# A cross-attention and soft-MoE kernel: the context turned on VectorE in 32x32 blocks instead of on TensorE

## The chip, the cores and the metric

One core of a Trainium2 chip runs the whole kernel in one launch. The metric is device time in microseconds (us): the median of three executions. TensorE (PE) multiplies and transposes into PSUM, VectorE (DVE) and ScalarE (ACT) work on PSUM and SBUF, GpSimd (POOL) on SBUF only, and SyncE (SP) issues transfers. All of them run in their own order and meet at semaphores.

## The reference, cut to what matters

```python
# x: (8, 56, 128), ctx_1024: (8, 1500, 128); 16 heads of 64
def _L0_xattn_ref(x, context, Wq, Wk, Wv, Wo):
    q = (x @ Wq).reshape(B, N, HEADS, DIM_HEAD)
    k = (context @ Wk).reshape(B, M, HEADS, DIM_HEAD)
    v = (context @ Wv).reshape(B, M, HEADS, DIM_HEAD)
    attn = jax.nn.softmax(jnp.einsum('bihd,bjhd->bhij', q, k) * SCALE, axis=-1)
    out = jnp.einsum('bhij,bjhd->bihd', attn, v).reshape(B, N, INNER)
    return out @ Wo
...
x = x + _L0_xattn_ref(_layernorm(x), ctx_1024, ...)   # attention over 1500 keys
x = x + _L0_ffn_ref(_layernorm(x), ...)               # soft mixture of 64 experts, 32 slots each
```

## The kernel before, in words

Keys are never projected: the weights of the query and key side are folded into one matrix per head, so that the scores of a batch are (folded queries) x (context turned). For a batch the 16 heads x 56 tokens are 896 rows, seven tiles of 128. The main loop runs over eight batches `b` and seven steps `t` of one tile each; `g = 7 b + t`. All float32 products are made of a high and a low part in the faster fp32r type: high x high, high x low, low x high. So the context is needed in four forms:

- `ctx_th`, `ctx_tl` (128 features x 1500 keys, high and low), for the scores, with keys along the free dimension;
- `ctx_nh`, `ctx_nl` (125 partitions x 12 chunks x 128 features), for the product of probabilities and context.

Both come from `ctx_raw`, which holds one batch in its natural layout: partition p has the 12 keys 12p to 12p + 11, 6144 bytes in one run (`ctx_v`). TensorE turns it in `turn_ctx`, three times four chunks, into a bank of `misc`; ScalarE copies the high part out (`hi_ctx`, L973), VectorE subtracts for the low part (`lo_ctx`, L1207), and the next four chunks wait for that (`ctxT_lo`). For batch `b + 1` this happens in steps 1, 2, 3 of batch `b`. GpSimd makes the natural parts in `split_ctx` (L408 and L412), one instruction each.

A step goes like this. TensorE makes the scores of tile g (L605 to L607), which must wait for the exponential of tile g - 1 since there is one scores buffer; turns two thirds of the probabilities of tile g - 1 (L617); does some chunks of the product with the context (`context_product`, L637 to L639, as `share` deals them out: groups of tiles (0,1), (2,3,4), (5,6)); turns the last third; and does the extras of `end_step`. VectorE takes row maxima (L1221, L1224), subtracts for the low part of the turned probabilities (`lo_probs`, L1231), inverts row sums (`invert`, L1240) and normalises a finished group (`normalise`, L1256). ScalarE copies high parts (`hi_probs`, L988), and takes the exponential (L995).

The one accumulator bank `acc` serves all groups, so a new group waits for `normalise` of the last (`oT_dve`). `normalise` needs the reciprocal row sums as a row on every partition, `rbc`. They take a path over DRAM, on SP's queue: `spread_rden` waits for `invert`, writes `rden_row` (L356), waits for it to land, waits for the normalisation before, and reads it back broadcast to 128 partitions (L359). VectorE normalises group 0 of batch b in step 6, group 1 in step 1 of batch b + 1, group 2 in step 3, each ahead of the row maxima of that step. SP runs in this order, with the load of the natural context between two spreadings:

```python
for b in range(B):
    if b > 0:
        spread_rden(NG * b, (b + 1) % 2, 2)
    spread_rden(NG * b + 1, b % 2, 0)
    if b + 2 < B:
        load_ctx(b + 2)
    spread_rden(NG * b + 2, b % 2, 1)
```

`load_ctx(b)` waits until `ctx_raw` is free, that is until TensorE has turned batch b - 1 and GpSimd has split it (`ctx_nat >= b`). The feed-forward part of the pairs of batches that are finished runs in between (`ffn_step`, `mid_step`, `dispatch_*`, `combine_*`), and its rest, with the experts, after the last batch.

## Time and profile before

| | |
|---|---|
| median of three executions | 452.91 us (450.67 to 454.25) |
| the profiled execution | 450.83 us, span 448.8 us |
| TensorE, VectorE, ScalarE, GpSimd busy | 96%, 76%, 55%, 31% of the span |
| granted TensorE clock | full, 1.0 in every slice |
| DMA | 19.05 MB, 42 GB/s over the span |

The span is the time from the first to the last instruction that the profiler recorded, and the execution is 2.0 us longer. Busy shares are of the whole span; the eight batches take the time from about 22 to 391 us, and the rest belongs to the start and to the experts. A row of the timeline has a start, a duration, the engine, the line, the operation, and in brackets how long the engine had been idle before it and what ended that.

### The profile page before, as it was taken

What the parts mean: (1) busy time and instruction counts of PE and PEld (TensorE: products, weight loads), DVE (VectorE), ACT (ScalarE), POOL (GpSimd) and SP (SyncE); (2) the same over time, 40 slices, a digit from 0 to 9 for tenths busy, and PEclk for the clock granted to TensorE, in tenths of its full rate; (3) what the DMA queues carried; (4) which work ended last, traced back from release to release, by engine and by line L of the source; (5) the groups of instructions that cost most, each with busy time, mean ns of one, the idle gap of its engine ahead of it and who ended that gap; (6) DMA issues with size and microseconds to landing.
All of it is one profiled execution on the core that took longest, in us unless ns stands there. A gap on an engine that the chain in (4) does not pass through costs nothing.

```text
span 448.8 us, 7525 instructions
## 1 busy us (share of the span) xinstructions
PE 429.8 (96%) x3038; PEld 392.6 (87%) x3038; DVE 339.1 (76%) x620; ACT 247.1 (55%) x422; POOL 137.5 (31%) x75
## 2 busy tenths in 40 slices
PE   1899999999999999999999999999999999899997
PEld 1788899999999999889999998989999888898986
DVE  2367776887587768757898778988997999668871
ACT  1375556665665356554665566646755654633641
POOL 1408100503050005030624043264440343446740
PEclk9999999999999999999999999999999999999999
DMA  7162110111001001110020011000100000576000
GB/s 224 52 143 34 65 25 12 13 68 19 13 13 70 19 12 14 68 19 13 9 73 19 12 13 69 19 1 15 14 18 2 12 13 23 90 193 183 1 3 20
DMA packets 15110, 19.05 MB, mean 42 GB/s; under 512 B 3954, under 2 KB 10882, under 8 KB 15076
## 3 DMA queue, kind: packets, MB, share of 16 engines
q1 hardware_dynamic: 13604, 16.48, 14.8%
q10 hardware_dynamic: 1472, 2.10, 1.6%
q8 instruction: 24, 0.39, 0.4%
q14 instruction: 10, 0.08, 0.1%
HBM read 18.32 MB, written 0.26 MB: 41 GB/s over the span
## 4 chain that ended last, share of the span: by engine, by line
PE 77%; DVE 10%; ACT 5%; DMA 3%; issue 2%; POOL 2%; POOLq 1%; SPq 0%
PE turned L617 15%; PE scores L605 8%; PE acc L639 8%; PE acc L637 8%; PE acc L638 8%; PE scores L607 8%; PE scores L606 8%; PE misc L654 3%; PE misc L549 3%; DMA ctx_raw<-in_ctx_dram 3%; DVE small L1221 2%; PE misc L679 2%; DVE pT_l L1231 2%; PE misc L543 2%; ACT prob L995 2%
## 5 line engine op out<-in xcount | busy, mean ns | idle before, releaser
L988 ACT CAST pT_h<-turned 125x512 fp32r<-125x512 f32 x168 | 94.9, 589 | 122.4 <-PE turned L617 121.7
L1231 DVE TENSOR_TENSOR pT_l<-turned,pT_h 125x512 fp32r<-125x512 f32 x168 | 112.2, 686 | 59.5 <-ACT pT_h L988 58.8
L1221 DVE TENSOR_REDUCE small<-scores 128x1 f32<-128x500 f32 x168 | 109.2, 674 | 10.2 <-PE scores L607 10.1
L617 PE MATMUL turned<-ident,prob 128*125 128x128 f32 x672 | 94.7, 276 | 2.8 <-DVE pT_l L1231 2.6
L617 PEld LDWEIGHTS turned<-ident,prob 128*125 128x125 f32 x672 | 87.5, 187 | 10.5 <-DVE pT_l L1231 4.3
L637 PE MATMUL acc<-pT_h,ctx_nh 125*128 125x256 f32 (+1 forms) x288 | 94.6, 329 | 0.0
L995 ACT ACTIVATE prob<-scores,small 128x1500 f32<-128x1500 f32 x56 | 84.9, 1516 | 14.5 <-DVE small L1224 14.5
L639 PE MATMUL acc<-pT_h,ctx_nl 125*128 125x256 f32 (+1 forms) x288 | 86.5, 300 | 0.0
L638 PE MATMUL acc<-pT_l,ctx_nh 125*128 125x256 f32 (+1 forms) x288 | 86.3, 300 | 0.0
L605 PE MATMUL scores<-ctx_th,qk_h 128*128 128x500 f32 x168 | 68.2, 406 | 0.7 <-DVE qk_l L1214 0.3
L607 PE MATMUL scores<-ctx_th,qk_l 128*128 128x500 f32 x168 | 65.3, 389 | 0.0
L606 PE MATMUL scores<-ctx_tl,qk_h 128*128 128x500 f32 x168 | 65.0, 387 | 0.0
L408 POOL TENSOR_TENSOR ctx_nh<-ctx_raw,zero 125x1536 fp32r<-125x1536 f32 x8 | 22.0, 2746 | 113.6 <-PE acc L639 98.9
L638 PEld LDWEIGHTS acc<-pT_l,ctx_nh 125*128 125x128 f32 x288 | 54.6, 190 | 0.0
L637 PEld LDWEIGHTS acc<-pT_h,ctx_nh 125*128 125x128 f32 x288 | 54.6, 189 | 0.0
L639 PEld LDWEIGHTS acc<-pT_h,ctx_nl 125*128 125x128 f32 x288 | 54.4, 189 | 0.0
L607 PEld LDWEIGHTS scores<-ctx_th,qk_l 128*128 128x128 f32 x168 | 31.5, 188 | 6.5
L605 PEld LDWEIGHTS scores<-ctx_th,qk_h 128*128 128x128 f32 x168 | 31.6, 188 | 6.3 <-issue 1.7
L606 PEld LDWEIGHTS scores<-ctx_tl,qk_h 128*128 128x128 f32 x168 | 31.7, 189 | 4.4
L458 POOL TENSOR_TENSOR logit<-logit,cmax 112x2048 f32<-112x2048 f32 (+1 forms) x5 | 18.5, 3704 | 34.1 <-DVE cmax L1287 32.5
L412 POOL TENSOR_TENSOR ctx_nl<-ctx_raw,ctx_nh 125x1536 fp32r<-125x1536 f32 x8 | 27.8, 3479 | 0.6
L419 POOL TENSOR_TENSOR qk_h<-qk_raw,zero 128x896 fp32r<-128x896 f32 x4 | 6.7, 1679 | 56.3 <-DVE qk_l L1214 56.3
(166 smaller groups left out, 537.3 us busy)
## 6 DMA issues: line engine op xcount, KB each, us to landing
ctx_raw<-in_ctx_dram SPq DMA_DIRECT2D x7, 750.0 KB
rbc<-rden_row SPq DMA_DIRECT2D x15, 128.0 KB, 3.4
rbc<-rden_row SPq DMA_DIRECT2D x8, 192.0 KB, 3.0
eb<-in_L_ffn_expert_b_dram SPq DMA_DIRECT2D x4, 256.0 KB, 6.1
ctx_raw<-in_ctx_dram SPq DMA_DIRECT2D x3, 250.0 KB
wq_sb<-in_L_xattn_Wq_dram ACTq DMA_DIRECT2D x1, 512.0 KB, 4.9
wk_sb<-in_L_xattn_Wk_dram ACTq DMA_DIRECT2D x1, 512.0 KB, 8.1
wv_sb<-in_L_xattn_Wv_dram ACTq DMA_DIRECT2D x1, 512.0 KB, 9.0
```

Of the source, the lines that this page charges most:

```text
L412: gp.tensor_tensor(ctx_nl[a][:, :, :], ctx_raw[:, :, :], ctx_nh[a][:, :, :].bitcast(F32), ALU.subtract).then_inc(ctx_nat, 1)
L605: mm(o, hi, ctx_th[a][:, keys], start=True, stop=False)
L606: mm(o, hi, ctx_tl[a][:, keys], start=False, stop=False)
L607: mm(o, lo, ctx_th[a][:, keys], start=False, stop=True).then_inc(scores_pe, 1)
L617: last = tr(turned[0:CK, m, 128 * c:128 * c + 128], prob[u][:, CK * j:CK * j + CK], ident[:, :])
L637: mm(o, ctx_nh[a][:, j, :], hi, start=(j == 0), stop=False)
L638: mm(o, ctx_nh[a][:, j, :], lo, start=False, stop=False)
L639: last = mm(o, ctx_nl[a][:, j, :], hi, start=False, stop=(j == NC - 1))
L988: nc.scalar.copy(pT_h[0:CK, PLACES[g // NT % 2][t], CPB * k:CPB * k + CPB, :], turned[0:CK, (KB * u + k) % 2, :].rearrange("p (c r) -> p c ...
L995: nc.scalar.activation(prob[u][:, :].rearrange("p (k w) -> p k w", k=KB), scores[:, :, 0:KW], ACT.Exp, bias=negmax[:, u:u + 1], accum_out= ...
L1221: m = v.tensor_reduce(bankmax[:, u, k:k + 1], scores[:, k, 0:KW], AX.X, ALU.max)
L1231: v.tensor_tensor(pT_l[0:CK, place, dst, :], turned[0:CK, (KB * u + k) % 2, :].rearrange("p (c r) -> p c r", c=CPB), pT_h[0:CK, place, dst ...
```

## The change

For batches 1 to 7 the context is turned in another way. A second load (`load_blocks`) brings the same batch once more from DRAM, laid out by blocks: partition 32e + k holds, for each block n of 32 keys, the 32 features 32e to 32e + 31 of key 32n + k. That is a run of 128 bytes for each partition and block. Eight DMAs do it: for each e one of 46 blocks (1472 runs) and one of the last block (32 runs), which overlaps the block before by four keys. VectorE's transpose of 32x32 blocks then gives the turned context, `ctx_tf`, in SBUF: four instructions for a batch, in steps 1, 2 and 3 of the batch before. ScalarE casts all 1500 columns to `ctx_th` in one instruction after step 4 (`hi_ctx`), and GpSimd subtracts for `ctx_tl` in one (`lo_ctx`), which lies ahead of `split_ctx` of the same batch in its order. The block loads of batches 2 to 7 are issued by ScalarE (`next_blocks`), behind that cast (batch 7's at the end of step 6 of batch 5); batch 1's by SP at the start.

Keys are now numbered straight, so the natural load of batches 1 to 7 takes another layout: partition p holds the keys 125j + p, 12 runs of 512 bytes (`ctx_c`). Batch 0 is as before. `ctx_tf` uses the memory of `ctx_tl`, and the block buffers lie in buffers of the feed-forward part, which adds two waits (`dispatch_shift(1)` for the last transposes, `logits(2, 0)` for the copies of the logits before).

```diff
+        ctx_tf = [at("ctx_tf0", [D, M], F32, tl0_at), at("ctx_tf1", [D, M], F32, tl1_at)]
+        BLK = 32
+        NB = -(-M // BLK)
+        blocks_at = [None] + [disp0_at + 1024] * 4 + [logit1_at] * 2 + [wqk_at]
...
+        ctx_c = ctx_1024.rearrange("b (j p) d -> b p j d", j=NC)
+
+        def load_blocks(eng, b):
+
+            for e in range(D // BLK):
+                cols = slice(BLK * e, BLK * e + BLK)
+                whole = ctx_1024[b, 0:BLK * (NB - 1), cols].rearrange("(n k) d -> k n d", k=BLK)
+                eng.dma_start(ctx_blk[b][cols, 0:NB - 1, :], whole).then_inc(blk_in, 16)
+                eng.dma_start(ctx_blk[b][cols, NB - 1, :], ctx_1024[b, M - BLK:M, cols]).then_inc(blk_in, 16)
...
             def load_ctx(b):
-                sp.wait_ge(ctxT_pe, KB * b)
+                sp.wait_ge(ctxT_pe, KB)
                 sp.wait_ge(ctx_nat, b)
-                sp.dma_start(ctx_raw[:, :, :], ctx_v[b]).then_inc(ctx_in, 16)
+                sp.dma_start(ctx_raw[:, :, :], ctx_c[b]).then_inc(ctx_in, 16)
...
+            load_blocks(sp, 1)
             load_ctx(1)
...
+            def lo_ctx(b):
+
+                pool.wait_ge(ctxT_hi, KB + b)
+                a = b % 2
+                gp.tensor_tensor(ctx_tl[a][:, :], ctx_tf[a][:, :], ctx_th[a][:, :].bitcast(F32),
+                                 ALU.subtract).then_inc(ctxT_lo, 1)
...
             def dispatch_shift(q):
                 pool.wait_ge(dmax_dve, 2 * (q + 1))
+                if q == 1:
+                    pool.wait_ge(ctxT_dve, B - 1)
...
-            split_ctx(1, 1)
...
+            lo_ctx(1)
+            split_ctx(1, 1)
+            lo_ctx(2)
             split_ctx(2, 0)
             split_qk(1)
+            lo_ctx(3)
             split_ctx(3, 1)
             root(1, 0, 1)
+            lo_ctx(4)
             split_ctx(4, 0)
...
             def end_step(b, t):
 
                 i, a, q = b // 2, b % 2, (b - 4) // 2
-                if 1 <= t <= 3 and b < B - 1:
-                    if t > 1:
-                        pe.wait_ge(ctxT_lo, KB * (b + 1) + t - 1)
-                    elif b == 2:
-                        pe.wait_ge(phi_cp, 1)
-                    elif b in (4, 6):
-                        pe.wait_ge(logit_act, LC * (q + 1))
-                    turn_ctx(b + 1, t - 1, 0)
...
                     if t == 0:
-                        pe.wait_ge(ctxT_lo, KB * (b + 1))
+                        pe.wait_ge(ctxT_lo, KB + b)
...
+            def hi_ctx(b):
+
+                act.wait_ge(ctxT_dve, b)
+                nc.scalar.copy(ctx_th[b % 2][:, :], ctx_tf[b % 2][:, :]).then_inc(ctxT_hi, 1)
+
+            def next_blocks(b):
+
+                if b == B - 1:
+                    act.wait_ge(qk_pe, 4 * PAIRS)
+                else:
+                    act.wait_ge(ctxT_dve, b - 1)
+                load_blocks(act, b)
...
-                if 1 <= t <= 3 and b < B - 1:
-                    hi_ctx(b + 1, 1 - a, t - 1, 0)
+                if t == 4 and b < B - 1:
+                    hi_ctx(b + 1)
+                if t == 4 and b < B - 3:
+                    next_blocks(b + 2)
+                if (b, t) == (B - 3, 6):
+                    next_blocks(B - 1)
...
+            def turn_blocks(b, part):
+
+                dst = ctx_tf[b % 2]
+                if part == 0:
+                    dve.wait_ge(blk_in, blocks_loaded(b))
+                    v.transpose(dst[:, M - BLK:M], ctx_blk[b][:, NB - 1, :]).then_inc(last_blk, 1)
+                n0, n1 = 16 * part, min(16 * part + 16, NB - 1)
+                if part == 2:
+                    dve.wait_ge(last_blk, b)
+                m = v.transpose(dst[:, BLK * n0:BLK * n1], ctx_blk[b][:, n0:n1, :].rearrange("p n d -> p (n d)"))
+                if part == 2:
+                    m.then_inc(ctxT_dve, 1)
...
-                    if 2 <= t <= 4 and b < B - 1 and not first:
-                        lo_ctx(b + 1, 1 - a, t - 2, 0)
+                    if 1 <= t <= 3 and b < B - 1:
+                        turn_blocks(b + 1, t - 1)
```

## Rows read from the trace of the kernel before

**Rows 1.** The page's chain of work that ended last, by engine.
```profile
PE 77%; DVE 10%; ACT 5%; DMA 3%; issue 2%; POOL 2%; POOLq 1%; SPq 0%
```

**Rows 2.** Timeline of TensorE's weight loads, end of step 1 of batch 2.
```profile
121.18 0.46 PEld L543 LDWEIGHTS misc<-ident,ctx_raw 125*128 125x128 f32 x4
...
121.61 0.47 PEld L662 LDWEIGHTS misc<-ident,phi_sb 128*128 128x128 f32 x4
```

**Rows 3.** Timeline of VectorE and ScalarE, step 1 of batch 3.
```profile
161.32 0.65 DVE L1256 TENSOR_TENSOR oT<-acc,rbc 128x384 f32<-128x384 f32 x1
...
163.95 1.51 ACT L995 ACTIVATE prob<-scores,small 128x1500 f32<-128x1500 f32 x1 [0.27 <-DVE small L1224]
```

**Rows 4.** TensorE's timeline: starts of step 4 and next step 2, batches 0, 2, 5.
```profile
45.35 0.46 PE L605 MATMUL scores<-ctx_th,qk_h 128*128 128x500 f32 x1
...
77.05 0.47 PE L605 MATMUL scores<-ctx_th,qk_h 128*128 128x500 f32 x1
...
133.80 0.47 PE L605 MATMUL scores<-ctx_th,qk_h 128*128 128x500 f32 x1
...
166.38 0.47 PE L605 MATMUL scores<-ctx_th,qk_h 128*128 128x500 f32 x1
...
271.75 0.48 PE L605 MATMUL scores<-ctx_th,qk_h 128*128 128x500 f32 x1
...
306.77 0.47 PE L605 MATMUL scores<-ctx_th,qk_h 128*128 128x500 f32 x1
```

**Rows 5.** Groups of instructions: busy us, mean ns of one, idle before, releaser.
```profile
L408 POOL TENSOR_TENSOR ctx_nh<-ctx_raw,zero 125x1536 fp32r<-125x1536 f32 x8 | 22.0, 2746 | 113.6 <-PE acc L639 98.9 <-DMA ctx_raw<-in_ctx_dram 14.8
L412 POOL TENSOR_TENSOR ctx_nl<-ctx_raw,ctx_nh 125x1536 fp32r<-125x1536 f32 x8 | 27.8, 3479 | 0.6
...
L1207 DVE TENSOR_TENSOR ctx_tl<-misc,ctx_th 128x500 fp32r<-128x500 f32 x24 | 16.0, 668 | 6.1 <-ACT ctx_th L973 6.1
```

**Rows 6.** Timeline of two DMA issues: start, time that the queue is held.
```profile
2.17 0.76 ACTq L958 DMA_DIRECT2D wo_sb<-in_L_xattn_Wo_dram  x1
...
24.49 0.82 SPq L365 DMA_DIRECT2D phi_sb<-in_L_ffn_phi_w_dram  x1
```

**Rows 7.** ScalarE's timeline, steps 4 and 5 of batches 2 and 4.
```profile
138.57 1.06 ACT L988 CAST pT_h<-turned 125x512 fp32r<-125x512 f32 x2
143.27 0.58 ACT L988 CAST pT_h<-turned 125x512 fp32r<-125x512 f32 x1 [3.64 <-PE turned L617]
...
231.45 1.93 ACT L1034 ACTIVATE disp<-disp 112x2048 f32<-112x2048 f32 x1
235.21 0.58 ACT L988 CAST pT_h<-turned 125x512 fp32r<-125x512 f32 x1 [1.83 <-PE turned L617]
```

**Rows 8.** SP's timeline in batch 2: the context load, then group 1's sums.
```profile
134.36 0.28 SPq L348 DMA_DIRECT2D ctx_raw<-in_ctx_dram  x1
144.69 0.32 SPq L356 DMA_DIRECT2D rden_row<-small  x1
```

**Rows 9.** Windows: length, engines' busy time, clock, DMA share of 16 engines, GB/s.
```profile
28.00:30.00 2.00, 2.00 (x12) 1.70 (x11) 1.61 (x4) 0.36 (x2) 0.00 (x0) 1.00 1.06 207
...
34.00:36.00 2.00, 2.00 (x15) 1.77 (x14) 2.00 (x5) 0.58 (x1) 0.86 (x1) 1.00 0.33 97
...
140.00:142.00 2.00, 2.00 (x14) 1.77 (x14) 0.98 (x2) 0.00 (x0) 0.00 (x0) 1.00 0.29 120
...
397.00:402.00 5.00, 5.00 (x49) 5.00 (x49) 3.22 (x6) 1.05 (x3) 1.32 (x2) 1.00 1.05 304
```

**Rows 10.** DMA issues of the page: count, KB each, median us to landing.
```profile
rbc<-rden_row SPq DMA_DIRECT2D x15, 128.0 KB, 3.4
...
rden_row<-small SPq DMA_DIRECT2D x15, 1.0 KB, 3.0
...
phi_sb<-in_L_ffn_phi_w_dram SPq DMA_DIRECT2D x1, 0.5 KB, 12.5
```

**Rows 11.** ScalarE's timeline, step 5 of batch 0: first work after step 4's copies.
```profile
52.86 0.60 ACT L973 CAST ctx_th<-misc 128x500 fp32r<-128x500 f32 x1
```

More of the change, by code:

```diff
@@ L133, in xattn_softmoe_kernel @@
         ctx_th1, t1_at = take("ctx_th1", [D, M], F32R)
-        ctx_tl1, _ = take("ctx_tl1", [D, M], F32R)
+        ctx_tl1, tl1_at = take("ctx_tl1", [D, M], F32R)
         qk_h1, _ = take("qk_h1", [D, HEADS, T], F32R)
@@ L137, in xattn_softmoe_kernel @@
         ctx_th0, t0_at = take("ctx_th0", [D, M], F32R)
-        ctx_tl0, _ = take("ctx_tl0", [D, M], F32R)
+        ctx_tl0, tl0_at = take("ctx_tl0", [D, M], F32R)
         qk_h0, _ = take("qk_h0", [D, HEADS, T], F32R)
@@ L156, in xattn_softmoe_kernel @@
         disp0, disp0_at = take("disp0", [PT, SLOTS])
-        logit1, _ = take("logit1", [PT, SLOTS])
+        logit1, logit1_at = take("logit1", [PT, SLOTS])
         _, stat0_at = take("stat0", [PT, 96])
@@ L181, in xattn_softmoe_kernel @@
         comb = logit
+        ctx_tf = [at("ctx_tf0", [D, M], F32, tl0_at), at("ctx_tf1", [D, M], F32, tl1_at)]
+        BLK = 32
+        NB = -(-M // BLK)
+        blocks_at = [None] + [disp0_at + 1024] * 4 + [logit1_at] * 2 + [wqk_at]
+        ctx_blk = [blocks_at[b] and at(f"ctx_blk{b}", [D, NB, BLK], F32, blocks_at[b]) for b in range(B)]
         stats_at = [stat0_at, stat1_at, t0_at + 2 * KB8, t0_at + 2 * KB8 + 384]
@@ L222, in xattn_softmoe_kernel @@
         ctxT_pe = sem("ctxT_pe")
+        blk_in = sem("blk_in")
+        ctxT_dve = sem("ctxT_dve")
+        last_blk = sem("last_blk")
         ctxT_hi = sem("ctxT_hi")
@@ L498, in _ @@
             dispatch_shift(0)
+            lo_ctx(5)
             split_ctx(5, 1)
@@ L501, in _ @@
             root(2, 1, 2)
+            lo_ctx(6)
             split_ctx(6, 0)
@@ L506, in _ @@
             dispatch_shift(1)
+            lo_ctx(7)
             split_ctx(7, 1)
@@ L534, in _, with turn_ctx @@
             tr = nc.tensor.transpose
-            def turn_ctx(b, k, m, first=False):
-                if first:
-                    pe.wait_ge(ctx0_in[k], 16)
-                else:
-                    pe.wait_ge(ctx_in, 16 * b)
+            def turn_ctx(k, m):
+                pe.wait_ge(ctx0_in[k], 16)
                 for c in range(CPB):
@@ L572, in _ @@
             turn_weight(wq_sb, 1, S1)
-            turn_ctx(0, 0, 1, first=True)
+            turn_ctx(0, 1)
             pe.wait_ge(xn_ready, 1)
@@ L577, in _ @@
             last.then_inc(setup_pe, 1)
-            turn_ctx(0, 1, 0, first=True)
+            turn_ctx(1, 0)
             pe.wait_ge(wk_in, 16)
@@ L582, in _ @@
             pe.wait_ge(ctxT_lo, 1)
-            turn_ctx(0, 2, 1, first=True)
+            turn_ctx(2, 1)
             pe.wait_ge(setup_dve, 3)
@@ L700, in mid_step @@
                     pe.wait_ge(x2nT_act, 3)
+                    pe.wait_ge(logit_act, 2 * LC)
                     logits(2, 0)
@@ L729, in end_step @@
                 if b in (3, 5) and t == 4:
-                    pe.wait_ge(ctxT_lo, KB * (b + 2))
+                    wait(pe, logit_act, LC * (i - 1))
                     pe.wait_ge(x2nT_act, i)
@@ L812, in half @@
                             head_products(wvT, wo_sb, 1, ACC)
[L813 to L815 removed]
+                            pe.wait_ge(qk_lo, 4)
                             head_products(wvT, wo_sb, 3, M1)
@@ L967, in copy_out, with hi_ctx0 @@
                 return nc.scalar.copy(dst, blocks4(bank(k))).then_inc(setup_act, 1)
-            def hi_ctx(b, a, k, m):
-                act.wait_ge(ctxT_pe, KB * b + (k + 1))
-                nc.scalar.copy(ctx_th[a][:, KW * k:KW * k + KW], misc[:, m, 0:KW]).then_inc(ctxT_hi, 1)
+            def hi_ctx0(k, m):
+                act.wait_ge(ctxT_pe, k + 1)
+                nc.scalar.copy(ctx_th[0][:, KW * k:KW * k + KW], misc[:, m, 0:KW]).then_inc(ctxT_hi, 1)
+            def hi_ctx(b):
[7 more added lines that the diff above has]
+                load_blocks(act, b)
             def hi_qk(i, r, m):
@@ L1113, in _ @@
             copy_out(2, wqT[:, 4:8, :], S1)
-            hi_ctx(0, 0, 0, 1)
-            hi_ctx(0, 0, 1, 0)
+            hi_ctx0(0, 1)
+            hi_ctx0(1, 0)
             copy_out(5, wkT[:, 4:8, :], T0)
-            hi_ctx(0, 0, 2, 1)
+            hi_ctx0(2, 1)
             copy_out(6, wqk[:, 0:8:2, :], T1, SCALE)
```

29 lines of the change are left out of this document (10 added, 19 removed).

## The prediction, made before the changed kernel had run

> **What bounds the kernel now.** I read the page's chain of work first: 77% of the chain that ended last is on TensorE [rows 1], and the page has it busy almost throughout. Work taken off TensorE is therefore worth its own time, as long as the other engines keep up. Next the timeline of one step (a "step" is one of the seven 128-row tiles of a batch, counted 0 to 6, batches 0 to 7). A group of four context transposes starts at 121.18 us and the next group of weight loads at 121.61: 0.43 us of TensorE's time, with no gap around it [rows 2]. Then the waits near the batch boundary, since that is where the change moves things: in step 1 of batch 3 VectorE normalises group 1 of batch 2 at 161.32, then takes the row maxima, and ScalarE's exponential starts 2.63 us after it, at 163.95 [rows 3]. The scores of step 2 overwrite the scores the exponential reads, and start at 166.38 [rows 4]. So that tile has about 0.9 us of slack (163.95 + 1.51 = 165.46). Last the DMA queues, because two new loads and one changed load use them.
>
> **What is saved.** In batches 1 to 6, steps 1 to 3 each lose four transposes: 18 x 0.43 = 7.7 us. In batch 0 the chain runs through VectorE and ScalarE; its copies of the low part (0.67 us each [rows 5], in steps 2, 3, 4) move to the middle of the step, where VectorE waits for the exponential. I count 0.6 us each, of which two lie ahead of the point I measure from below: 1.2 us.
>
> **VectorE.** 21 subtractions of 0.668 us go, 21 block transposes of 448 or 512 columns and 7 of 32 come. No row shows a VectorE transpose. The nearest is the subtraction that goes, 0.668 us for 500 columns [rows 5]; I bound it by half of that and by double. I take the same rate, 0.65 us, and 0.15 for the short one, so VectorE's work stays within 0.1 us a batch, and it stands where VectorE waits for the exponential anyway. At double it would cost perhaps 0.3 us in the fullest steps, some 2 us in all; at half it gives nothing, as VectorE is not the bound there. The Trainium skill (Vector Engine (DVE) Microarchitecture Reference, section 3.8) says that the transpose sustains one element per cycle per lane; by that the 512 columns would be an estimated 0.53 us plus overhead. No run here shows it yet.
>
> **ScalarE.** 21 copies out of PSUM become 7 casts of 1500 columns from SBUF, about 1.5 us each (2048 columns took 1.93 us [rows 7]), at the end of step 4. Behind each stand eight DMA issues on ScalarE's queue. Nearest rows: 0.76 and 0.82 us for loads of several runs per partition [rows 6], 0.28 and 0.32 us for plain ones [rows 8]. I take 4 x (0.75 + 0.32) = 4.3 us; bounds 2.3 and 6.6. Queued behind them are the next high-part copy (143.27 in batch 2, after 3.64 us without work) and, in batch 4, a 1.93 us exponential that starts at 231.45 while the next copy starts at 235.21 [rows 7]. With issues and cast overlapping, the copy is late by roughly 0.4 us in batch 2, 2.1 in batch 4, 1.2 to 1.5 in batches 0, 1, 3, and nothing in batch 5, where the next step has room. Alone that would be 6.7 us, since these steps have four chunks of product, which just cover the copy.
>
> **GpSimd and the SP queue; here the change hurts.** The low part of batch b+1 goes onto GpSimd *ahead* of the split of batch b+1. In batch 2:
> - Step 4 starts at 133.80 [rows 4]; ScalarE's last copy of it ends at 138.57 + 1.06 = 139.63 [rows 7], 5.8 us into the step. The cast ends at 7.3.
> - The low part on GpSimd: 3.48 us for 1536 columns [rows 5], 3.4 for 1500: 10.7. Then the split, 2.75 + 3.48 [rows 5]: 17.1.
> - SP's next load of the natural context waits for that split. In the old kernel it was issued at 134.36 [rows 8], 0.6 into step 4; now at 17.1.
> - Directly behind it on SP stands the spreading of the reciprocal sums of group 1, which was issued at 144.69, ten us *after* the load. Now it is issued just after it.
> - The load keeps five engines of sixteen busy: the DMA share is 0.29 while it runs, with 120 GB/s, until about 142 [rows 9]. A transfer queued behind such a load waits for those five: the phi load, 1 MB issued at 24.49 directly behind batch 1's context load, took 12.5 us to land [rows 6, 10]; the share fell from 1.06 to 0.33, five engines, for its last part [rows 9].
> - The new load has 1500 runs of 512 bytes, 300 for each of five engines. The expert load's runs are 512 bytes: 304 GB/s on sixteen engines [rows 9] is 27 ns a run and engine. 300 x 27 = 8.1 us, and 0.9 us before the first byte: it ends at 26.1 after step 4's start. Bounds: 21 ns (120 GB/s on five engines) and 40 ns (207 GB/s, the phi load), so 6.4 to 12 us.
> - The 1 KB of reciprocals lands in 3.0 us from its issue, the broadcast back in 3.4 [rows 10]. The first is already issued, so +2.1, then +3.4: 31.6.
> - VectorE wants it at 161.32, which is 27.5 after step 4's start. It waits 4.1 us, in order, ahead of the row maxima. The exponential ends 2.6 + 1.5 later, and the scores of step 2 start 0.2 after: 35.9.
>
> Before, those scores started 166.38 - 133.80 = 32.6 after step 4's start: +3.3. The same two rows of each batch (the first, third and last of six are in [rows 4]) give spans of 31.7, 32.0, 32.6, 35.0, 32.9 and 35.0 us for batches 0 to 5. In batch 0 ScalarE is free only 7.5 into the step [rows 11], so 37.6 stands against 31.7. The shifts: +5.9, +3.9, +3.3, +0.9, +3.0, +0.9 = +17.9 us. They contain the late copies of ScalarE (the late broadcast outlasts them, except for 0.3 in batch 3) and the lost transposes of step 1. Batches 6 and 7 have no such load.
>
> The engine count is where the Trainium skill bears on this (DMA: Bandwidth & Descriptors, "Why a DMA increments its semaphore by 16 and not by 1"): a transfer takes the largest number of engines up to 16 that divides the slowest dimension of both sides. For 125 partitions that is 5, also in the new layout; the share of 0.29 to 0.33 [rows 9] agrees for the old one (five sixteenths are 0.31). With sixteen engines the forecast would be the first rival below.
>
> **The block loads.** A batch is 6016 runs of 128 bytes, 376 an engine. The rows of 512-byte runs, 27 and 40 ns [rows 9], bound it above, and a quarter of 27 for a quarter of the bytes bounds it below: 3 to 15 us. Batches 2 to 6 have over 20 us. Batch 7's is issued at about 292 and wanted at about 305, batch 1's waits behind batch 0's load until about 17 and is wanted at 31: up to 25 or 30 ns nothing, at 40 about 3 us each. I take none.
>
> **Sum.** +17.9 - 1.2 - 12 x 0.43 (steps 2 and 3) = +11.5; with 0.3 of ScalarE and a few tenths where VectorE becomes the tighter engine, +12. The profiled execution took 450.83 us (span 448.8), 2.1 under the median of 452.91. 450.8 + 12 = 463 for such an execution, 465 as a median.
>
> **Rivals.**
> 1. *The broadcast comes in time*: the new load spreads over sixteen engines, or the small transfers don't queue behind it. Then it is ready 5.6 us earlier, at 26, and only batch 0 is short by 1 us. For it: the new source pattern has never run. Against: the share rows and the phi load. With cheap issues on ScalarE (2.6 us, as the 0.32 us rows, late copies of about 1 us in all): 450.8 - 9.5 + 2 = 443, median 445. This is the case on the other side; it decides from a broadcast ready before 27.5.
> 2. *The same, with ScalarE's issues at 0.75 us for the wide ones*: -9.5 + 6.7 + 1 = -2, median 451.
> 3. *Dearer runs*: 40 ns for 512 bytes adds 3.9 us to each of six batches: +23, and some 3 us of late blocks: 488 to 491. The row for it is the phi load, which however ran beside another load.
> 4. *Eight DMAs in a row are more than the queue takes*, and ScalarE is held while blocks move. The loads of the start and of phi never stand more than four in a row on a queue. Four wide transfers of 2.5 us would hold it 10 us a batch: about 495.
>
> **Chances.** Forecast 0.62 (456 to 476), rival 1 0.15, rival 2 0.10, rival 3 0.09, rival 4 0.04. The measurement can tell about 1%, 4.5 us. Rival 1 is faster by over 1%, rival 2 within it, the rest slower; with a little of the forecast's lower tail within: 0.16, 0.12, 0.72. The range from 447 to 487 leaves out most of rival 1 and the upper cases, about 2 in 10.
>
> **What would show it.** In the changed kernel's waits: VectorE's normalisation waiting for the broadcast in step 1 of batches 1 to 6, some 4 us, less in batches 4 and 6; SP's context load issued 17 us into step 4's span; DMA share about 0.31 for some 8 us with the reciprocals landing only after it, 10 us or more instead of 3. ScalarE's eight issues summing to about 4.3 us; transposes near 0.65 us; TensorE busy about 11 us less (84 transposes) in a longer span. The prediction is wrong if normalisation does not wait: then either the engine count or the queue order was misread. It is too low if VectorE waits for blocks.

## The result, and the profile after

The changed kernel takes 479.76 us (median of four executions, 478.53 to 481.13) against 453.52 us before in the same comparison: the ratio is 1.059, with a 95% interval of 1.0535 to 1.065. The profiled executions stand at 481.13 us (span 479.3) and 450.83 us (span 448.8), so this pair differs by 30.5 us of span; the pair is accounted for below. The forecast had +12. (Single executions of the kernel before differ by up to 4 us, and the profiled one is among its fastest; by the medians the change costs 26.2 us.)

The chain of work that ended last, by engine; against [rows 1] TensorE has gone from 77% to 34%, and waiting for issues, transfers and other engines has come in:

```profile
PE 34%; issue 18%; DVE 16%; DMA 9%; ACT 9%; POOL 8%; ACTq 4%; POOLq 1%; SPq 0%
```

To see where, I took from TensorE's timeline the first scores row of each step in both kernels (L605 before, L640 after, as in [rows 4]) and subtracted the lengths of the steps. The first scores of all start at 26.16 us instead of 22.43 (+3.7). Then, after minus before, in us:

| batch | step 0 | 1 | 2 | 3 | 4 | 5 | 6 | sum |
|---|---|---|---|---|---|---|---|---|
| 0 | +0.3 | 0.0 | 0.0 | -0.6 | -0.8 | +0.8 | 0.0 | -0.3 |
| 1 | 0.0 | **+6.7** | 0.0 | -0.4 | -0.1 | **+1.7** | 0.0 | +7.9 |
| 2 | 0.0 | **+5.8** | -0.3 | -0.4 | +0.1 | +1.1 | 0.0 | +6.3 |
| 3 | 0.0 | +1.8 | -0.4 | -0.4 | -0.1 | +1.3 | 0.0 | +2.1 |
| 4 | 0.0 | -0.4 | -0.4 | +0.3 | +0.1 | **+3.7** | 0.0 | +3.4 |
| 5 | 0.0 | -0.2 | -0.4 | -0.4 | -0.1 | 0.0 | 0.0 | -1.1 |
| 6 | **+7.2** | +1.4 | -0.4 | +0.1 | +0.1 | 0.0 | 0.0 | +8.4 |

Batch 7 and everything behind it are unchanged. The steps that shrink by 0.4 are those that lost a group of transposes [rows 2]. The rest are four places, and each has its rows.

**Step 1: the broadcast is late.** GpSimd's timeline at the end of batch 0 (low part, then the two halves of the split), SP's, and VectorE's and TensorE's in step 1 of batch 1, then of batch 2:

```profile
57.12 3.41 POOL L441 TENSOR_TENSOR ctx_tl<-ctx_tf,ctx_th 128x1500 fp32r<-128x1500 f32 x1 [12.69 <-ACT ctx_th L1000]
60.48 2.75 POOL L430 TENSOR_TENSOR ctx_nh<-ctx_raw,zero 125x1536 fp32r<-125x1536 f32 x1
63.31 3.49 POOL L434 TENSOR_TENSOR ctx_nl<-ctx_raw,ctx_nh 125x1536 fp32r<-125x1536 f32 x1
...
66.87 0.30 SPq L369 DMA_DIRECT2D ctx_raw<-in_ctx_dram  x1
67.21 5.99 SPq L377 DMA_DIRECT2D rden_row<-small  x1
76.87 0.32 SPq L380 DMA_DIRECT2D rbc<-rden_row  x1
...
81.57 0.66 DVE L1307 TENSOR_TENSOR oT<-acc,rbc 128x384 f32<-128x384 f32 x1 [5.98 <-DMA rbc<-rden_row]
82.38 0.55 PE L672 MATMUL acc<-pT_h,ctx_nh 125*128 125x256 f32 x1 [4.68 <-DVE oT L1307]
87.21 0.62 PE L640 MATMUL scores<-ctx_th,qk_h 128*128 128x500 f32 x1
...
132.84 0.66 DVE L1307 TENSOR_TENSOR oT<-acc,rbc 128x384 f32<-128x384 f32 x1 [5.16 <-DMA rbc<-rden_row]
133.65 0.55 PE L672 MATMUL acc<-pT_h,ctx_nh 125*128 125x256 f32 x1 [3.45 <-DVE oT L1307]
139.19 0.61 PE L640 MATMUL scores<-ctx_th,qk_h 128*128 128x500 f32 x1
```

The context load is issued the moment the split ends, 66.87, and the reciprocals directly behind it. The 5.99 on that row is not the transfer: it is how long the *issue* holds SP's queue, where the same instruction took 0.32 in [rows 8]. The load's own runs of 512 bytes are on the engines from 0.94 to 9.23 us after its issue. The broadcast is there at 81.57, 14.7 us after the load was issued, and VectorE and then TensorE stand idle for it. VectorE waits so in three batches only: 5.98 us in step 1 of batch 1, 5.16 in batch 2, 2.44 in batch 3. In batches 4, 5 and 6 its wait there is 0.08, 0 and 0.

**What the stall does to TensorE's clock.** Windows over step 1 of batch 2 (columns: length; busy time of PE, PEld, DVE, ACT, POOL; granted clock; DMA share; GB/s):

```profile
128.00:130.00 2.00, 2.00 (x14) 1.77 (x13) 0.00 (x0) 0.20 (x1) 0.00 (x0) 1.00 0.11 43
130.00:132.00 2.00, 0.20 (x2) 0.01 (x1) 0.00 (x0) 0.39 (x1) 0.00 (x0) 1.00 0.18 56
132.00:134.00 2.00, 0.35 (x1) 0.38 (x2) 1.16 (x2) 0.00 (x0) 0.00 (x0) 0.66 0.00 0
134.00:136.00 2.00, 2.00 (x11) 2.00 (x11) 1.97 (x6) 0.51 (x1) 0.00 (x0) 0.50 0.08 28
136.00:138.00 2.00, 2.00 (x11) 2.00 (x11) 1.16 (x4) 1.57 (x3) 0.00 (x0) 0.50 0.11 38
138.00:140.00 2.00, 2.00 (x11) 1.92 (x10) 0.99 (x2) 1.01 (x2) 0.00 (x0) 0.63 0.03 8
```

In and after 3.45 us of idleness the engine is granted 0.50, the lower of its two levels (1.2 of 2.4 GHz), and works at it for about 6 us. From the normalisation to the next scores it takes 139.19 - 132.84 = 6.35 us here and 5.64 in batch 1. In batch 3, where VectorE waits only 2.4 us and the column stays at 1.00, it is 4.3.

**Step 5: ScalarE's issues.** ScalarE's timeline in batch 4, the last of eight issues and the exponential behind them, which stood at 231.45 before, directly behind its predecessor [rows 7]:

```profile
250.11 0.32 ACTq L324 DMA_DIRECT2D ctx_blk<-in_ctx_dram  x1
...
254.12 0.82 ACTq L325 DMA_DIRECT2D ctx_blk<-in_ctx_dram  x1
254.99 1.91 ACT L1069 ACTIVATE disp<-disp 112x2048 f32<-112x2048 f32 x1 [2.33 <-issue]
...
314.34 1.52 ACTq L325 DMA_DIRECT2D ctx_blk<-in_ctx_dram  x1
...
316.36 5.78 ACTq L325 DMA_DIRECT2D ctx_blk<-in_ctx_dram  x1
...
323.87 2.51 ACTq L325 DMA_DIRECT2D ctx_blk<-in_ctx_dram  x1
326.41 0.59 ACT L1058 COPY logit<-misc 112x512 f32<-112x512 f32 x1 [11.85 <-issue]
```

The eight take 4.83 us (250.11 to 254.94). L324 is the wide issue, 1472 runs, and L325 the one of 32 runs behind it; even unhindered the small one takes longer (0.71 to 0.91 us, the wide one 0.32 to 0.45).

In batch 4 TensorE has 1.98 us without work behind this, and the clock falls there too, which is part of the +3.7:

```profile
258.00:260.00 2.00, 1.84 (x12) 1.84 (x13) 2.00 (x3) 1.84 (x4) 1.92 (x2) 0.73 0.00 0
260.00:262.00 2.00, 2.00 (x11) 2.00 (x11) 1.97 (x2) 0.00 (x0) 2.00 (x1) 0.50 0.03 8
```

**Step 0 of batch 6: ScalarE held.** The second part of the fence with ScalarE's issues is batch 7's blocks, issued by ScalarE at 314 while SP's context load (issued at 310.93) is in flight. Two of the small issues, each behind a wide one, are held 5.78 and 2.51 us, and ScalarE does nothing for 11.85 us. VectorE, which needs its copies, waits 9.02, and TensorE 6.07 and runs at 0.50 afterwards.

**The start.** SP's timeline (batch 1's blocks right behind batch 0's context) and TensorE's; two rows of before follow for comparison:

```profile
3.10 10.01 SPq L325 DMA_DIRECT2D ctx_blk<-in_ctx_dram  x1
...
17.69 1.07 PE L578 MATMUL misc<-ident,ctx_raw 125*128 125x125 f32 x4 [0.53 <-DMA ctx_raw<-in_ctx_dram]
...
19.92 0.42 PE L600 MATMUL turned<-wkT,wqT 64*128 64x128 f32 x1
```

```profile
16.80 0.84 PE L543 MATMUL misc<-ident,ctx_raw 125*128 125x125 f32 x4
...
18.79 0.27 PE L565 MATMUL acc<-wkT,wqT 64*128 64x128 f32 x1
```

The third part of batch 0's context comes 0.9 us later. The rest of the +3.7 is TensorE's clock: from the first of the L600 rows to the first scores it takes 7.5 us, where it took 4.9 before, and the same product has rows of 0.42 us against 0.27. The clock column prints 1.00 for both, but it has nothing to go by there. The trace's first entry on the clock, a rise to 1.00, is at 26.83 us in the changed kernel and at 17.27 in the kernel before. That the rows ahead of it are at the lower level shows by their length. Sixteen matmuls of one shape, first in the changed kernel's start and in the start of the kernel before, then in the changed kernel at a granted 0.50 (15 records) and at 1.00:

```profile
22.73 3.75 PE L584 MATMUL misc<-xnT,wqk 128*128 128x112 f32 x16
```

```profile
20.11 2.01 PE L549 MATMUL misc<-xnT,wqk 128*128 128x112 f32 x16 [0.28 <-issue]
```

```profile
259.13 3.36 PE L689 MATMUL misc<-oT,wvo 128*128 128x112 f32 x15
...
353.57 1.94 PE L689 MATMUL misc<-oT,wvo 128*128 128x112 f32 x16
```

Why the clock rises 9.6 us later in one kernel than in the other stays open: none of the runs below settles it.

### The profile page after: what moved, and what is told of

Read it like the earlier page. It is cut to its first block, busy times and chain, and to the rows that moved or that the text cites. A ratio compares the mean times of both kernels' runs of the same rounds, so it can differ in the third digit from the quotient of the medians.

```text
span 479.3 us, 7399 instructions
## 1 busy us (share of the span) xinstructions
PE 436.6 (91%) x2954; PEld 396.6 (83%) x2954; DVE 339.0 (71%) x627; ACT 245.8 (51%) x408; POOL 161.0 (34%) x82
## 4 chain that ended last, share of the span: by engine, by line
PE 34%; issue 18%; DVE 16%; DMA 9%; ACT 9%; POOL 8%; ACTq 4%; POOLq 1%; SPq 0%
PE turned L652 6%; DVE small L1272 5%; DVE pT_l L1282 5%; DMA rden_row<-small 4%; ACT prob L1030 4%; PE scores L640 3%; ACTq L325 3%; DMA ctx_raw<-in_ctx_dram 3%; PE scores L642 3%; PE scores L641 3%; PE acc L672 3%; PE acc L674 3%; PE acc L673 3%; ACT pT_h L1023 3%; PE misc L689 3%
## 5 line engine op out<-in xcount | busy, mean ns | idle before, releaser
L652 PE MATMUL turned<-ident,prob 128*125 128x128 f32 x672 | 96.5, 280 | 16.6 <-DVE pT_l L1282 16.2
L652 PEld LDWEIGHTS turned<-ident,prob 128*125 128x125 f32 x672 | 88.8, 190 | 26.0 <-DVE pT_l L1282 20.6
L672 PE MATMUL acc<-pT_h,ctx_nh 125*128 125x256 f32 (+1 forms) x288 | 96.7, 336 | 9.2 <-DVE oT L1307 9.2
L674 PE MATMUL acc<-pT_h,ctx_nl 125*128 125x256 f32 (+1 forms) x288 | 88.3, 307 | 0.0
L673 PE MATMUL acc<-pT_l,ctx_nh 125*128 125x256 f32 (+1 forms) x288 | 88.1, 306 | 0.0
L441 POOL TENSOR_TENSOR ctx_tl<-ctx_tf,ctx_th 128x1500 fp32r<-128x1500 f32 x7 | 23.9, 3413 | 176.1 <-ACT ctx_th L1000 176.1
L640 PE MATMUL scores<-ctx_th,qk_h 128*128 128x500 f32 x168 | 69.2, 412 | 1.0 <-ACT prob L1030 0.7
L672 PEld LDWEIGHTS acc<-pT_h,ctx_nh 125*128 125x128 f32 x288 | 56.3, 196 | 9.7 <-issue 9.7
L673 PEld LDWEIGHTS acc<-pT_l,ctx_nh 125*128 125x128 f32 x288 | 56.4, 196 | 0.0
L674 PEld LDWEIGHTS acc<-pT_h,ctx_nl 125*128 125x128 f32 x288 | 56.2, 195 | 0.0
L640 PEld LDWEIGHTS scores<-ctx_th,qk_h 128*128 128x128 f32 x168 | 32.6, 194 | 7.2 <-issue 2.0
L468 POOL TENSOR_TENSOR disp<-logit,dmax 112x2048 f32<-112x2048 f32 x3 | 11.0, 3650 | 40.3 <-DVE ctx_tf L1257 25.1
```

Source lines behind the costliest of these rows:

```text
L640: mm(o, hi, ctx_th[a][:, keys], start=True, stop=False)
L652: last = tr(turned[0:CK, m, 128 * c:128 * c + 128], prob[u][:, CK * j:CK * j + CK], ident[:, :])
L672: mm(o, ctx_nh[a][:, j, :], hi, start=(j == 0), stop=False)
L673: mm(o, ctx_nh[a][:, j, :], lo, start=False, stop=False)
L674: last = mm(o, ctx_nl[a][:, j, :], hi, start=False, stop=(j == NC - 1))
```

## The experiments

All are edits of the changed kernel unless said otherwise. "Excess" is the length of a step over before, as in the table above. Each time stands beside runs of the kernel before (medians 453.5 to 454.0).

### e1_spread_first: SP's two orders exchanged

```diff
                 spread_rden(NG * b + 1, b % 2, 0)
+                spread_rden(NG * b + 2, b % 2, 1)
                 if b + 2 < B:
                     load_ctx(b + 2)
-                spread_rden(NG * b + 2, b % 2, 1)
```

> The changed kernel with one change of order on SP: the spreading of group 1's reciprocals goes ahead of the load of the natural context. Theory A (the broadcast of group 1 is late because it queues behind the context load): step 1 of batches 1 to 3 and 6 loses its excess over the old kernel (6.7, 5.8, 1.8 and 1.4 us in the trace of the changed kernel) and the steps 1 of all six batches show the 0.4 us of the transposes saved; no normalisation waits for the broadcast for more than 1 us. That is 17 to 18 us: 462 us from 479.8. The 7.2 us in step 0 of batch 6 stay, since batch 7's blocks still collide with a context load. Theory B (the DMA issues on ScalarE are the main cost, and the wait for the broadcast is only where it shows): the lost time moves to the next wait, and the time stays above 474.

459.72 us, ratio 1.016 [1.0105, 1.021]. Step 1 of batches 1 to 3 went from +6.7, +5.8, +1.8 to -0.35, -0.43, -0.35: the whole stall there, and the clock's fall with it, were the order on this queue. Steps 5 kept +0.8, +1.6, +1.2, +1.2, +3.9, step 0 of batch 6 kept +5.2 and its step 1 +0.6, where the saving was expected too. Two lines are worth 20 us.

### e2_split_first: GpSimd's split ahead of its low part

```diff
-            lo_ctx(2)
             split_ctx(2, 0)
+            lo_ctx(2)
```

(for each batch, with the other extras in place)

> The changed kernel with GpSimd's order turned round: the split of a batch goes ahead of its low part, so that SP's context load is issued again in step 4 or before. Theory A: the broadcast is in time in all batches, worth 17 to 18 us, and batch 7's blocks no longer meet a context load, worth 7 more: 455. Theory B (a queue that issues is held while a context load fills the rings): now every block load of batches 2 to 6 is issued some 5 us behind a context load instead of 5 us ahead of one, so ScalarE is held about 5 us in step 4 of each batch and the gain is eaten: 475 to 485.

488.59 us, ratio 1.079 [1.073, 1.086]: worse, as the second theory had it, and by more than its 475 to 485. The steps 1 and step 0 of batch 6 are repaired, but the context load now goes out just ahead of ScalarE's block loads, and steps 5 have +7.3, +7.9, +7.9, +7.3, +9.1. Each of the five has a gap of 5.6 to 7.4 us in TensorE's work and 6.8 us at a granted 0.50. SP's and ScalarE's timeline in batch 4:

```profile
253.99 0.28 SPq L369 DMA_DIRECT2D ctx_raw<-in_ctx_dram  x1
...
258.17 1.38 ACTq L325 DMA_DIRECT2D ctx_blk<-in_ctx_dram  x1
...
260.06 5.60 ACTq L325 DMA_DIRECT2D ctx_blk<-in_ctx_dram  x1
...
268.14 1.91 ACT L1069 ACTIVATE disp<-disp 112x2048 f32<-112x2048 f32 x1 [7.78 <-issue]
```

The load is on SP's queue and the held issue on ScalarE's. What they share, as far as the trace shows it, are the engines that move the data. It is not that only one queue can issue at a time: in the changed kernel SP's issue is held from 311.65 to 318.51, and ScalarE gets three issues through meanwhile. The start is that of the changed kernel, yet here the clock is up at 18.68 and the first scores are 1.1 us late, not 3.7.

### e3_load_16_engines: the context load cut into 112 + 13 partitions

```diff
-                sp.dma_start(ctx_raw[:, :, :], ctx_c[b]).then_inc(ctx_in, 16)
+                sp.dma_start(ctx_raw[0:112, :, :], ctx_c[b][0:112]).then_inc(ctx_in, 16)
+                sp.dma_start(ctx_raw[112:CK, :, :], ctx_c[b][112:CK]).then_inc(ctx_in, 16)
```

> The changed kernel with the natural context load in two parts, 112 and 13 partitions, in place of one of 125; the order of everything stays. Theory A (the load keeps five engines busy for 8.3 us, since it has 125 partitions): 112 partitions are spread over sixteen engines, the load takes about 3 us, the DMA share is near 1 while it runs, the broadcast comes 5 us earlier, and the waits for it fall from 6.0 to about 1 us: some 13 us, and several us less of the hold in step 0 of batch 6: 460 to 465. Theory B (the broadcast is late because of the 1500 short runs as such, on whatever engines): no more than 3 us are gained.

461.84 us, ratio 1.021 [1.015, 1.026]. Step 1 has +3.1 in batch 1, its saving in batches 2 to 5, and +0.4 in batch 6; step 0 of batch 6 falls from +7.2 to +2.3. A window of the load shows what the cut does, 0.36 and 107 GB/s in the changed kernel (first), 0.86 and 182 here:

```profile
70.00:72.00 2.00, 2.00 (x16) 1.96 (x15) 1.78 (x4) 1.20 (x2) 0.00 (x0) 1.00 0.36 107
```

```profile
70.00:72.00 2.00, 2.00 (x16) 1.96 (x15) 1.78 (x4) 1.14 (x2) 0.00 (x0) 1.00 0.86 182
```

So the number of engines set the length of the load, as the prediction read it. What is left in batch 1 is plain queueing without a held issue: the reciprocals are issued at 68.07 in 0.37 us and the broadcast can only follow at 73.87.

### e4_start_later: batch 1's blocks after batch 0's context

```diff
+            for k in range(KB):
+                sp.wait_ge(ctx0_in[k], 16)
             load_blocks(sp, 1)
```

> The changed kernel with batch 1's block load issued by SP only when the three parts of batch 0's context have landed (about 17 us). Theory A (the 3.7 us by which the first scores start later, 26.2 against 22.4, come from the block load that shares the engines with the first context parts and the weights, after which TensorE's matmuls run longer for some microseconds): the first scores start near 22.5 us again and the whole kernel gains 3 to 4 us, 476. Theory B (the start is slower for another reason, or VectorE then waits for batch 1's blocks in step 1 of batch 0 for as long): no change, 479 to 481.

476.67 us, ratio 1.053 [1.047, 1.058]; the first scores come 0.25 us later than before's instead of 3.7. The transfers account for about 1 us of that (the third part is turned at 16.97 instead of 17.69); the rest is TensorE's clock, which is up at 17.62 here, so that the L600 rows are at 0.27 us. In this profile step 5 of batch 4 has +2.1 in place of +3.7: TensorE's gap is the same 2.0 us there, but the clock stays at 1.00 behind it.

### e11_change_again: the changed kernel once more

No edit.

> The changed kernel once more, unaltered, for the start: its profile showed TensorE's rows between 18 and 26 us of the span 1.57 times as long as before's (0.42 against 0.27 us), the kernel with the later start showed them at 0.27. Theory A (the longer rows belong to this kernel): first scores again 3.7 us late, 478.5 to 481. Theory B (they belong to single executions): first scores 1.1 us late in this profile, and a time of 477.

479.52 us, first scores again 3.8 us late, rows again at 0.42, the clock's rise at 26.57. So the late rise is no accident of one execution. It is not fixed by what the kernel does at the start either. The profile of e2 has the changed kernel's start and its rise at 18.68; two more pairs with the same start are 17.58 and 26.28 (e6b, e5b), and 15.17 and 23.63 (e7b, e10).

### e5b_three_repairs: spreads first, cut loads, late start

The diffs of e1, e3 and e4 in one kernel, no other edit.

> The changed kernel with three edits at once: SP's second spread of the denominators stands ahead of the context load, batch 1's blocks are issued after batch 0's context has landed, and the context loads of batches 1 to 7 are cut into 112 + 13 partitions. Theory A (the queue hold and the start are separate losses that add): 479.8 - 20.1 - 3.1 - about 3 = 453 to 454; steps 5 keep their excess over before of 0.8, 1.6, 1.2, 1.2 and 3.9, since ScalarE still issues the blocks. Theory B (the repairs overlap, the same loss taken away twice): 458 or more.

456.77 us, ratio 1.007 [1.0046, 1.010], 3 us over theory A and just under B. Steps 5 are as A has them (+0.9, +1.6, +1.3, +1.2, +3.7) and step 0 of batch 6 is down to +0.9. The 3 us are the start: batch 0's context lands early, but TensorE's clock rises only at 26.28 again, and the first scores come 2.4 us late.

### e9_issues_on_sp: spreads first, all block loads on SP

To the first experiment:

```diff
                     load_ctx(b + 2)
+                    if b + 2 < B - 1:
+                        sp.wait_ge(ctxT_dve, b + 1)
+                    else:
+                        sp.wait_ge(qk_pe, 4 * PAIRS)
+                    load_blocks(sp, b + 2)
...
-                if t == 4 and b < B - 3:
-                    next_blocks(b + 2)
-                if (b, t) == (B - 3, 6):
-                    next_blocks(B - 1)
```

> The kernel with the second spread ahead of the context load (459.7), and in it all block loads on SP, behind the context load, none on ScalarE; GpSimd's order is that of the change. Theory A (the excess of 0.8 to 3.9 us at steps 5, and what is left at step 0 of batch 6, are ScalarE's eight issues and the hold of its queue): steps 5 lose it, 459.7 - 8.7 - 5 = 446, 444 to 449. Theory B (the excess is the other work at step 5, VectorE's transposes or the cast that came late): steps 5 stay, 457 to 461.

459.53 us, the time of theory B by the mechanism of theory A. Steps 5 lose their excess in every batch (-0.4, 0.0, 0.0, 0.0, 0.0) and step 0 of batch 6 too, 14 us. But step 2 of batches 1 and 2 is now 7.1 and 3.4 us longer than before, and in batches 3 and 5 it is 0.6 and 0.3 longer instead of 0.5 and 0.4 shorter. SP's timeline, then VectorE's first transpose of batch 2's blocks:

```profile
66.50 0.30 SPq L369 DMA_DIRECT2D ctx_raw<-in_ctx_dram  x1
66.85 6.17 SPq L324 DMA_DIRECT2D ctx_blk<-in_ctx_dram  x1
73.07 3.08 SPq L325 DMA_DIRECT2D ctx_blk<-in_ctx_dram  x1
...
84.13 0.21 DVE L1253 STREAM_TRANSPOSE ctx_tf<-ctx_blk 128x32 f32<-128x32 f32 x1 [7.08 <-DMA ctx_blk<-in_ctx_dram]
```

The hold has moved to the blocks, and now VectorE waits for them.

### e6b_blocks_on_sp: context load early and cut, all blocks on SP

The diffs of e2, e3 and e4 together, the block issues on ScalarE taken out as in e9, and the blocks between context load and second spread:

```diff
                 if b + 2 < B:
                     load_ctx(b + 2)
+                if b + 2 < B - 1:
+                    sp.wait_ge(ctxT_dve, b + 1)
+                    load_blocks(sp, b + 2)
                 spread_rden(NG * b + 2, b % 2, 1)
+                if b + 2 == B - 1:
+                    sp.wait_ge(qk_pe, 4 * PAIRS)
+                    load_blocks(sp, b + 2)
```

> The context load is released early (GpSimd's split ahead of its low part), the loads are cut into 112 + 13 partitions, batch 1's blocks start late as before, and all wide block loads stand on SP's queue, none on ScalarE's. Theory A (ScalarE's eight issues are what is left at step 5, and no DMA that anyone waits for stands behind a held issue): steps 5 lose their excess, 440 to 445. Theory B (the excess at step 5 is not ScalarE's issuing but the transposes on VectorE or the late copy): it stays, 450 to 454.

445.19 us, ratio 0.982 [0.9775, 0.9865]. No step has an excess over 0.2 us; the batches sum to -7.8.

### e7b_blocks_on_sp_ctx0_16: and batch 0's three parts cut too

```diff
-                sp.dma_start(ctx_raw[:, chunks, :], ctx_v[0][:, chunks, :]).then_inc(ctx0_in[k], 16)
+                sp.dma_start(ctx_raw[0:112, chunks, :], ctx_v[0][0:112, chunks, :]).then_inc(ctx0_in[k], 16)
+                sp.dma_start(ctx_raw[112:CK, chunks, :], ctx_v[0][112:CK, chunks, :]).then_inc(ctx0_in[k], 16)
```

> As the kernel with the blocks on SP, and batch 0's context parts are cut into 112 + 13 partitions too. Theory A (the first context parts bound the start): 2 to 3 us less than that kernel, the first scores at 19 to 20 us from the span's start. Theory B (TensorE's work bounds the start): within 1 us of it.

440.64 us, ratio 0.974 [0.969, 0.9785], the best of all. The first scores start at 19.64, 3.0 us earlier than in e6b. The profiled pair differs by 1.5 us more, all of it behind the last batch: in both kernels TensorE is idle for 1.4 us there, but in e6b's profile the clock is at 0.50 for 3.4 us afterwards and in this one it is not. The windows behind it, e6b first:

```profile
383.00:385.00 2.00, 2.00 (x12) 2.00 (x11) 1.60 (x2) 2.00 (x2) 0.00 (x0) 0.50 0.00 0
```

```profile
380.00:382.00 2.00, 2.00 (x19) 2.00 (x18) 1.52 (x2) 2.00 (x2) 0.00 (x0) 1.00 0.00 0
```

The chain is TensorE's again, at 72%:

```profile
PE 72%; DVE 15%; ACT 6%; issue 2%; DMA 2%; POOL 2%; POOLq 1%; SPq 0%
```

### e8b_before_load_16: the kernel before with cut loads

The kernel before with the diffs of e3 and e7b, for all eight batches.

> The kernel before, with all its context loads (batch 0's three parts too) cut into 112 + 13 partitions. Theory A (only the start is bound by a context load; later its loads are hidden): the first scores come 2 to 3 us earlier, nothing else moves, 450 to 451.5. Theory B (the transfer of later batches was part of the time too, so that the gain of the best repaired kernel is the cut's and not the transposes'): 445 or less.

448.53 us, ratio 0.988 [0.986, 0.991]. That is 1.5 us under theory A's range and above theory B's. The start gains 1.9 us and no step moves by more than 0.02. The clock rises at 16.72 here and at 15.17 in the best kernel, and the first scores are 0.9 us apart (20.57 and 19.64). What remains of the repaired kernel's lead is the change's own: its span is 438.3 against 447.0, and 7.7 of these 8.7 us lie in the batches.

### e10_scalar_issues: the best kernel with ScalarE issuing again

The best kernel with `load_blocks(sp, ...)` out of SP's loop and the change's own `next_blocks` calls back in ScalarE's `end_step`.

> The kernel of 440.6 with the block loads of batches 2 to 7 issued by ScalarE at the end of step 4 again, as the change has them; context loads stay early and cut. Theory A (the eight issues stand ahead of the exponential of the next chunk whatever the queue does): steps 5 of batches 0 to 4 lose 1.2 to 1.6 and 3.7 us, 8.9 together, 449 to 451. Theory B (with the context load early and on 16 engines the issues are hidden): 441 to 444.

452.11 us, ratio 0.998 [0.9945, 1.001], executions from 449.8 to 456.0. Steps 5 of batches 0 to 4 lose 2.6, 1.7, 1.5, 1.1 and 2.4 against the best kernel, 9.3 together where 8.9 was expected, although nothing holds the queue:

```profile
235.94 0.92 ACTq L325 DMA_DIRECT2D ctx_blk<-in_ctx_dram  x1
236.91 1.92 ACT L1073 ACTIVATE disp<-disp 112x2048 f32<-112x2048 f32 x1 [2.65 <-issue]
```

The median is 1 us above A's range. In the profiled execution the start is 2.4 us later (the clock rises at 23.63), step 0 of batch 0 takes 0.8 longer, and 1.5 lie behind the last batch, where the clock is at 0.50 for 3.4 us from 392.27 as in e6b's profile.

### e12_half_loads: the load in two halves of six chunks, still on 5 engines

```diff
-                    load_ctx(b + 2)
+                    load_ctx(b + 2, 0, NC // 2)
                 spread_rden(NG * b + 2, b % 2, 1)
+                if b + 2 < B:
+                    load_ctx(b + 2, NC // 2, NC)
```

> The changed kernel with each context load cut by chunks into two DMAs of six, still on 5 engines: the first where the load stood, the second behind SP's second spread. 150 runs of 512 B an engine are then ahead of the spread's first DMA instead of 300. Theory A (a later issue goes through once about 65 runs an engine are left: 6.0 us is 300 - 65 runs at 27 ns): the issue is held 2.3 us; steps 1 of batches 1 and 2 lose some 3.7 us less each, step 1 of batch 3 nothing, 466 to 471. Theory B (a held issue takes some 6 us whatever is ahead of it): it stays at 4 us, all that the half load lasts, or more, and the time at 474 or more.

468.54 us, ratio 1.032 [1.0295, 1.035]; step 1 has +1.6, -0.4, -0.3 in batches 1 to 3. SP's timeline:

```profile
67.14 0.30 SPq L369 DMA_DIRECT2D ctx_raw<-in_ctx_dram  x1
67.48 2.09 SPq L377 DMA_DIRECT2D rden_row<-small  x1
73.19 0.32 SPq L380 DMA_DIRECT2D rbc<-rden_row  x1
73.60 0.30 SPq L369 DMA_DIRECT2D ctx_raw<-in_ctx_dram  x1
73.95 4.23 SPq L377 DMA_DIRECT2D rden_row<-small  x1
```

Half the runs ahead, and the hold is 2.09 us instead of 5.99. The difference, 3.9, is 150 runs an engine at 26 ns. A fixed time is excluded. What decides is how many runs of the load are still to come. Counted in the traces, 569 are left of the first half when its follower gets through and 557 of the second, whose follower is held 4.23 us, and 528 of the 1500 in the changed kernel (67.21). All holds of SP's queue directly behind a context load on five engines, in this and the other profiles, end with 486 to 582 left, about 97 to 116 an engine. The load cut into 112 + 13 partitions has no more than 96 an engine (84 and 12) to begin with, and its follower was not held (e3). Step 0 of batch 6 got worse (+9.2), where the second half now lies across batch 7's block issues.

## Why the prediction was wrong

The direction, the place of the first loss and its mechanism were right, and 479.8 us lies in the wide range of 447 to 487. But it lies outside the 456 to 476 that the forecast itself was given, and the size, +12 for a measured +30.5 on the profiled pair (26.2 by the medians), was wrong. Three of its terms failed: the way from the stall to the next scores was reckoned at full clock; ScalarE's issues in batch 5 were taken to cost nothing and were held 12.4 us behind a load on another queue; and the start was put at nothing. Step by step:

- **GpSimd to SP to broadcast: right.** Context load issued 17.1 us after step 4's start: 18.0, 17.0, 17.4, 17.0, 17.4, 17.0. From the load to the broadcast 14.5: 14.7, 16.0 and 13.9 where VectorE waited. The load ended 9.2 us after its issue (9.0 reckoned). Five engines at 27 ns a run: the share was 0.29 to 0.40 while the load ran, and the cut into 112 + 13 partitions took it to 0.86. By that, the Trainium skill's rule for the number of engines (DMA: Bandwidth & Descriptors, "Why a DMA increments its semaphore by 16 and not by 1") holds in the new layout too: 5 divides 125, 16 divides 112. What I did not see is *how* the follower waits: its issue holds the queue, not only its data.
- **The shift from step 4 to the next step 2** (terms of +5.9, +3.9, +3.3, +0.9, +3.0, +0.9): measured +6.7, +7.4, +2.9, +0.8, +3.6, +8.5. Four of six hold within 0.8 us, two of them by luck: from batch 3 to 4 and from 4 to 5 VectorE waited 0.08 and 0 us for the broadcast, and the shift is ScalarE's late copy (+1.3 and +3.7 in step 5), not the queue on SP. The sign "VectorE waits in step 1 of batches 1 to 6" came true in batches 1 to 3. Two are mis-sized:
  - *Batch 1 to 2, 3.5 us.* "The exponential ends 2.6 + 1.5 later, and the scores start 0.2 after" takes VectorE and ScalarE as the bound behind the stall, 4.3 us. With TensorE at the lower clock it took 6.35 us; at 1.00, in batch 3, it took the 4.3 reckoned. The broadcast was also 1.5 us later than reckoned.
  - *Batch 5 to 6, 7.6 us.* "Nothing in batch 5, where the next step has room" counted ScalarE's eight issues at 4.3 us. They took 12.4 us (313.98 to 326.38), because a context load was in flight. Rival 4 had this mechanism, a queue that holds ScalarE, but with another cause (its own four wide transfers) and for every batch. I had looked for what stands behind SP's load on SP's queue only, not on ScalarE's.
- **"Batch 1's waits behind batch 0's load ... I take none": wrong by 3.7 us.** The price asked was that of the blocks; the one paid was by batch 0's context, whose transfers the blocks share (about 1 us), and by TensorE's clock, which rose at 26.83 us instead of 17.27 (about 2.6). Why it rose later is not shown.
- **The remaining steps**, +0.5 - 1.2 - 5.2 = -5.9: measured -3.2. The transposes did save 0.43 each where the table shows -0.4. In step 3 of batches 4 and 6, and in step 2 of batch 1, which begins at the lower clock, they saved nothing; in step 3 of batches 4 and 6 that is so in the repaired kernels too (+0.2), for a cause that no run shows. Batch 0 gave 0.3 ahead of its step 4, where 1.2 was counted.
- Together: 3.5 + 7.6 + 3.7 + 2.7, and +1.0 from the four other shifts, are 18.5, the difference between +12 and +30.5.
- **VectorE's transpose and the issues: right.** 681 ns on average for 512 columns (0.65 taken), 0.20 for 32, so 1.0 ns for a further column. The Trainium skill's one element per cycle and lane (Vector Engine (DVE) Microarchitecture Reference, section 3.8) gave an estimated 0.53 us plus overhead, and the trace agrees. Eight issues 4.8 us (4.3), with the two prices the other way round: 0.45 us for a wide one, 0.72 for the small one behind it. The late copies cost 1.2 to 1.7, 1.1 and 3.7 us instead of 1.2 to 1.5, 0.4 and 2.1. Of the 3.7 some 1.6 is TensorE's clock: where it stays at 1.00 the step has +2.1 (e4) and +2.4 (e10), where it falls +3.1 to +3.9 (six profiles).
- **The rivals.** The first, "the broadcast comes in time", was put at 445 for a kernel in which ScalarE's issues are cheap. Such a kernel is the one with blocks on SP: 445.2. With ScalarE's issues it was put at 451; the kernel that has them measured 452.1 (it also has the cut start). This one is neither: something queues behind its narrow load. The two hits are partly luck. The batches of the first save 7.8 us and not 9.5, and the 2 us of issues in its sum are not on ScalarE at all; the second's batches sum to +2.3 where -2 was reckoned, and its start is 0.4 us early.
- **"TensorE busy about 11 us less": wrong.** It is busy 436.6 us in the changed kernel and 429.8 before, with 84 instructions fewer (2954 and 3038), since part of its work runs at the lower clock.

## What to carry to other kernels

Before a small transfer that somebody waits for is left behind a large one, look at what the large one occupies: reordering two entries on one queue was worth 20 us here, and keep an engine that also computes from issuing transfers while another queue's narrow load is in flight. Price a stall of TensorE with its aftermath, by rows at the lower clock, and price each issue on ScalarE at full length wherever ScalarE's next instruction is on the chain. When a change loses, repair its queue orders before judging it: the same transposes, with the transfers in another order, give 440.6 us, where the kernel before with the same cut loads takes 448.5.
